# Zero rows and zero weights around the 48 rows of the shift-16 pairs, in a fused three-layer CIN kernel

## The reference

```python
def _L0_rec_ref(inputs, W1, b1, W2, b2, W3, b3, fc_W, fc_b):
    X0 = inputs.reshape(-1, NUM_FIELDS, EMBED_DIM)        # 64 x 32 x 64
    Xi = X0
    pools = []
    for W, b in ((W1, b1), (W2, b2), (W3, b3)):
        out_ch = W.shape[0]                               # 128
        m = Xi.shape[1]                                   # 32, then 128
        Wr = W.reshape(out_ch, NUM_FIELDS, m)
        Xi = jnp.einsum('bhd,bmd,ohm->bod', X0, Xi, Wr) + b[None, :, None]
        pools.append(Xi.sum(axis=-1))
    concat = jnp.concatenate(pools, axis=-1)
    return concat @ fc_W.T + fc_b
```

## Time and profile before

| | |
|---|---|
| median of three runs | 107.69 us |
| the profiled execution's own time | 108.17 us |
| its span in the profile | 106.4 us |
| PE busy | 81.1 us (76%), 303 matmuls |
| DVE busy | 62.7 us (59%) |
| POOL busy | 38.5 us (36%) |
| ACT busy | 34.8 us (33%) |
| chain that ended last | PE 69%, DVE 16%, DMA 5%, ACT 4%, issue 3% |

### The profile page before, as it was taken

The page is one execution under the profiler, slowest core; times in us unless marked ns, Lnnn a source line. Parts: engine busy times, 40 slices in busy tenths (PEclk is TensorE's granted clock), DMA queues, the critical chain, the costliest instruction groups (busy, mean ns, idle before and its releaser), DMA issues.

```text
span 106.4 us, 960 instructions
## 1 busy us (share of the span) xinstructions
PE 81.1 (76%) x303; PEld 60.8 (57%) x303; DVE 62.7 (59%) x87; ACT 34.8 (33%) x66; POOL 38.5 (36%) x31
## 2 busy tenths in 40 slices
PE   0042692006999999934999999999999999999921
PEld 0031570004899879934767766776677666866710
DVE  0239999998600029959995999829987011020072
ACT  4008400019500277462809722076190200201100
POOL 2033099930700079955602309245062204022000
PEclk9999999755555555555589999999999999999998
DMA  3959999920599998971074643700000000000000
GB/s 94 402 135 353 419 431 419 434 117 0 112 110 125 393 404 250 116 310 65 0 219 176 194 200 89 305 3 0 0 6 0 0 0 0 0 0 0 0 0 0
DMA packets 3464, 15.64 MB, mean 147 GB/s; under 512 B 516, under 2 KB 644, under 8 KB 2180
## 3 DMA queue, kind: packets, MB, share of 16 engines
q1 hardware_dynamic: 3460, 15.59, 45.0%
HBM read 14.27 MB, written 0.00 MB: 134 GB/s over the span
## 4 chain that ended last, share of the span: by engine, by line
PE 69%; DVE 16%; DMA 5%; ACT 4%; issue 3%; SPq 0%; DVEq 0%
PE x_ps L538 27%; PE a_ps L538 27%; PE a_ps L599 11%; DMA rep<-xr 5%; DVE w_sb L180 5%; DVE v L476 2%; DVE z_ps L406 2%; ACT feat L313 2%; DVE feat L415 2%; DVE rows_sb L437 1%; PE a_ps L526 1%; ACT v_all L313 1%; ACT a_sb L313 1%; DVE total L509 1%; DVE total L506 1%
## 5 line engine op out<-in xcount | busy, mean ns | idle before, releaser
L538 PE MATMUL x_ps<-feat,w_hi 128*128 128x512 f32 x64 | 27.9, 495 | 2.4 <-DMA fc_all<-fc 2.4
L406 DVE TENSOR_TENSOR z_ps<-rep 128x512 f32<-128x512 f32 x24 | 21.2, 910 | 13.2 <-DMA rep<-xr 12.3
L538 PE MATMUL a_ps<-feat,a_hi 128*128 128x512 f32 x64 | 21.9, 403 | 0.0
L251 POOL TENSOR_TENSOR z_pool<-rep 128x512 f32<-128x512 f32 x8 | 14.9, 1858 | 15.3 <-DMA rep<-xr 13.6
L538 PEld LDWEIGHTS x_ps<-feat,w_hi 128*128 128x128 f32 x64 | 15.1, 236 | 7.0 <-DMA fc_all<-fc 2.8
L313 ACT ACTIVATE feat<-z_ps 128x512 fp32r<-128x512 f32 x24 | 13.9, 592 | 14.1 <-DVE z_ps L406 14.1
L285 POOL TENSOR_TENSOR x<-x 128x512 f32<-128x512 f32 x6 | 8.5, 1413 | 23.5 <-DVE x L466 23.5
L466 DVE SCALAR_TENSOR_TENSOR x<-a_ps,vec,x 128x512 f32<-128x512 f32 x8 | 6.0, 744 | 18.5 <-PE a_ps L538 18.5
L538 PE MATMUL x_ps<-feat,w_lo 128*128 128x512 f32 x32 | 15.6, 488 | 1.6 <-DVE w_tail L456 1.6
L415 DVE TENSOR_TENSOR feat<-z_ps,feat 128x512 fp32r<-128x512 f32 x24 | 16.0, 682 | 1.0 <-ACT feat L313 0.8
L599 PEld LDWEIGHTS a_ps<-v_all,w_sb 128*128 128x128 f32 x60 | 14.6, 331 | 1.6 <-issue 0.9
(11 more groups left out here) (66 smaller groups left out, 69.0 us busy)
## 6 DMA issues: line engine op xcount, KB each, us to landing
rep<-xr SPq DMA_DIRECT2D x8, 1024.0 KB, 5.4
w_sb<-w SPq DMA_DIRECT2D x4, 512.0 KB, 8.8
w_sb<-w SPq DMA_DIRECT2D x2, 1024.0 KB, 13.5
w_sb<-w SPq DMA_DIRECT2D x1, 560.0 KB, 3.8
tail<-z_hi SPq DMA_DIRECT2D x2, 256.0 KB, 5.4
xp<-x SPq DMA_DIRECT2D x1, 512.0 KB, 8.1
lin<-xp_lo SPq DMA_DIRECT2D x1, 512.0 KB, 6.7
xa<-x SPq DMA_DIRECT2D x1, 256.0 KB, 6.9
```

Source lines behind the costliest of these rows:

```text
L251: nc.gpsimd.tensor_tensor(z_pool[:, c % 2, :], rep[:, c % 2, left, :], rep[:, c % 2, right, :], ALU.mult).then_inc(zp_done, 1)
L406: nc.vector.tensor_tensor(z_ps[:, k, :], rep[:, c % 2, left, :], rep[:, c % 2, right, :], ALU.mult).then_inc(z_done, 1)
L538: last = nc.tensor.matmul(bank, w, f, **kw)
```

## The change

The three SBUF tensors of the shift-16 pairs, `tail`, `w1_tail` and `a_tail`, grow from 48 to 128 partitions. POOL writes zeros into all three ahead of its first product. The copies and DMAs of the real data still write rows 0 to 47. The matmuls of L559 and L572 are written as before, over the whole tensors, and so now have 128 rows, 80 of them zero by zero. ACT waits for two of the memsets before it copies a tail weight, SP for all three before its DMAs into `tail`.

```diff
-        tail = sb("tail", [3 * HALF, CHUNKS, N], f32r)
+        tail = sb("tail", [P, CHUNKS, N], f32r)
-        w1_tail = sb("w1_tail", [3 * HALF, M], f32r)
+        w1_tail = sb("w1_tail", [P, M], f32r)
-        a_tail = sb("a_tail", [3 * HALF, M], f32r)
+        a_tail = sb("a_tail", [P, M], f32r)
...
+        tail_zero = sem("tail_zero")
...
                 sp.wait_ge(done, 1)
+                sp.wait_ge(tail_zero, 3)
                 sp.dma_start(tail[row * HALF:(row + 1) * HALF, :, :].bitcast(f32),
...
+            nc.gpsimd.memset(w1_tail[:, :].bitcast(f32), 0.0).then_inc(tail_zero, 1)
+            nc.gpsimd.memset(a_tail[:, :].bitcast(f32), 0.0).then_inc(tail_zero, 1)
+            nc.gpsimd.memset(tail[:, :, :].bitcast(f32), 0.0).then_inc(tail_zero, 1)
             pairs(0)
...
-                copy(tl[:, :], a_ps[1][0:3 * HALF, 0:M]).then_inc(wt_hi, 1)
+                act.wait_ge(tail_zero, 2)
+                copy(tl[0:3 * HALF, :], a_ps[1][0:3 * HALF, 0:M]).then_inc(wt_hi, 1)
```

## The result

The changed kernel takes 102.83 us (median of four runs, 102.33 to 105.63) against 107.97 us before (107.32 to 108.32, four runs). The ratio, taken without the execution of 105.63 us, is 0.9515, with an interval of 0.9442 to 0.9589; the medians differ by 5.1 us. Forecast were 101.9 us and a range of 100.3 to 103.5.

A forecast was written before the change was run, and what follows sets the result against it. From about 55 us on, PE's matmul count times the start-to-start step was taken as the bound. Savings of 5.2 + 0.65 - 0.05 = 5.8 us gave 101.9 us against the median of 107.69, range 100.3 to 103.5.

The forecast's parts named there:

- The tail's price and its cause: PE at the higher clock: each 48-row tail costs 0.40 us extra by draining PE on entry and leaving; padding removes both.
- the end of a group: Rival at PE's tails: the gap belongs to closing a PSUM group, so nothing changes, 107.7 us; chance 0.04.
- The tails at the higher clock, 5.2 us: 14 tails on PE behind the clock's rise: twelve at 0.40 us and two at 0.2 us, together 5.2 us saved.
- The allowance of 0.2 for the tail ahead of L624: Tail at 93.68 us, before L624's one-row matmuls: only 0.2 us saved, since those may charge for the switch themselves.
- The tails at the lower clock, 0.65 us: Two early tails, layer 1 of chunk 1 and L572: 0.7 us of PE time saved, 0.65 us taken as reaching the end.
- each waiting for the one before: Chain behind L572: L599 matmuls, ACT's copies, DVE's rows, transposes and PE follow in turn, passing PE's early gain on.
- The memset, nothing: POOL's three memsets, 3.4 us for `tail`, end at about 5.3 us inside idle time lasting to 7.04 us: no cost.
- The rival's mechanism: A dear memset makes POOL's first product late and DVE's chain slip; chance of costing over a microsecond 0.06.
- The new wait at `a_product(2)`, 0.05 us: PE, come forward, may wait there for DVE's product of chunk 0: 0.35 us at most, 0.05 us taken.
- The sum: Whole kernel: 5.2 + 0.65 - 0.05 = 5.8 us saved, giving 101.9 us against the median.
- the clock's rise: PE's clock rising up to 3 us earlier or later against its work: 100.5 to 103.3 us, most of the range.

The follow-up runs named there:

- middle48: Kernel before with 48-row tails moved inside their group, in the a products and in layer 1 from chunk 2 on: 107.94 us, before 107.57 in that series.
- pad64: Changed kernel with the three tensors 64 rows high instead of 128: 107.95 us.
- memset_only: Changed kernel with its 128-row zeroed tensors, but tail matmuls reading only rows 0 to 47: 107.32 us against 107.31 before, ratio 1.001.
- again: Changed kernel run once more without any edit, for an undisturbed profile: 102.82 us, against 107.31 before in the same series.
- memset3: Changed kernel with the memset of the tail tensor done three times in a row: 106.39 us.
- y_late: Changed kernel with the output's six small matmuls (L624, L625) issued behind the last a product, not ahead of the last layer-1 product: 102.32 us.
- again2: Changed kernel run a third time without any edit, next to a 96-row version: 102.39 us.
- cold48: Changed kernel with the two early tails (layer 1 of chunks 0 and 1) back to 48 rows: 102.85 us.
- a_only: Changed kernel with only the eight tails of the a products at 128 rows, those of layer 1 at 48: 104.42 us.
- rep_early_y_late: As y_late, with SP also issuing the replicas of chunk 2 ahead of its DMAs into tail and xp: 101.27 us, ratio to before 0.9348.

## Why the prediction was right, point by point

**The tail's price and its cause.** Right. 0.40 us a tail was forecast from four steps, and the four steps fell from 1.31 to 0.91 us. The cause, rows and not the end of a group, is shown by `middle48` and `pad64` from both sides, and `memset_only` leaves nothing above its noise for the rest of the change. That it is a drain of PE is the likeliest reading and no more.

**The tails at the higher clock, 5.2 us.** Right. The stretch holds thirteen of the fourteen tails and fell by 4.91 us. The fourteenth, of the layer-1 product of chunk 2, has 0.3 of its 0.40 us ahead of the stretch (0.09 on entry and 0.20 in the step behind): 5.2 us in all. That product itself, 4.81 us before and 4.39 in `again`, measures nothing of the kind: it took from 3.58 (`memset3`) to 5.10 us (`y_late`) with full rows, by where the clock rose. The allowance of 0.2 for the tail ahead of L624 was right too. The step behind this tail fell from 0.42 only to 0.33 us (91.51 to 91.84 in the first trace), not to 0.23, because L624 brings a switch of its own; with the entry that is 0.18.

**The tails at the lower clock, 0.65 us.** This is the term that was mis-sized. The premise, that they would cost 0.7 us of PE's time up to the small matmuls, held: `again2`, at the low rate in the trace from 25 to 45 us like the kernel before, has the clean pattern of 1.28 us around its tails, and its last small matmuls start 0.88 us earlier (44.26 against 45.14), 0.72 of it gained by the end of the two tails (38.43 against 39.15). Before and in `again2`:

```profile
45.14 1.04 PE L599 MATMUL misc_ps<-v_all,w_sb 128*128 128x33 f32 x4
```

```profile
44.26 1.04 PE L605 MATMUL misc_ps<-v_all,w_sb 128*128 128x33 f32 x4
```

What failed is "each waiting for the one before". ACT's copies no longer wait for PE but stand right behind ACT's own feature, which waits for DVE and the replicas:

```profile
44.13 0.60 ACT L318 ACTIVATE feat<-z_ps 128x512 fp32r<-128x512 f32 x1 [1.08 <-DVE z_ps L412]
44.63 0.97 ACT L318 ACTIVATE a_sb<-a_ps 128x495 f32<-128x495 f32 x2
```

In the chain the copies start at 44.73 us against 45.37, so 0.64 of the 0.88 are left. DVE's last low part of chunk 2 then meets POOL's product (45.57 to 46.84 us) and takes longer. Before and in `again2`:

```profile
46.96 0.69 DVE L415 TENSOR_TENSOR feat<-z_pool,feat 128x512 fp32r<-128x512 f32 x1 [1.08 <-ACT feat L313]
```

```profile
46.22 1.17 DVE L421 TENSOR_TENSOR feat<-z_pool,feat 128x512 fp32r<-128x512 f32 x1 [0.33 <-ACT feat L318]
```

It starts 0.74 us earlier and takes 0.48 more, and the transposes start only 0.27 us earlier (49.04 against 49.31). So the term was 0.3 us where PE went at the low rate, on one pair of traces. Where it went faster from 28 to 33 us, the early tails were worth nothing: `pad64` and `cold48`, which have the switches, start their transposes at 49.00 and 48.98 us, `again`, which has not, at 49.01.

**The memset, nothing.** Right: 3.51 us against 3.4 worked out from the slope of two short ones, 1.8 us of cover left. `memset_only` times the whole edit at a ratio of 1.001 (0.9942 to 1.0079). The rival's mechanism is real, as `memset3` shows, but my price for it, microsecond for microsecond, was too low: 3.2 us at the transposes where 1.9 were due.

**The new wait at `a_product(2)`, 0.05 us.** Of the right order, 0 to 0.2 us, depending on where the clock rises. In `again` there is no wait: DVE's product of chunk 0 is over at 60.54 us (59.81 + 0.73) and PE's matmul follows its predecessor in a clean step at 61.17. In `again2` the clock rose earlier and PE was there 0.6 us sooner, while DVE's product ended at 60.56 (59.83 + 0.73). PE's matmul started at 60.62, and this wait is the 0.16 us by which the stretch of `again2` is longer. In `memset3` it cost 0.2 us. So DVE did not come forward with PE there, and a faster PE would meet this limit next.

**The sum.** 5.2 us at the higher clock and 0.3 at the lower make 5.5; against the 5.8 forecast, it is the early tails that are missing. The spans of single traces say less, since the place of the clock's rise is in them: against 106.4 us before, `again` is 5.5 us shorter and `again2` 6.1. The medians give 5.1 in the first series, 4.5 and 5.3 in the two others with this kernel; the kernel before varies from 105.4 to 109.1 us by itself. The traced execution of it, 108.17 us, is a long one with POOL first at 13.2 us; no trace of a short one is kept, so whether the order accounts for these stays open.

**The spread.** The range named the clock's rise as its main part. That is one of two. The other, which I did not see, is the order of DVE and POOL at 13.3 us. That all three medians of this kernel (102.83, 102.82, 102.39) lie inside the range is thus in part luck: no traced execution of it had DVE first, and in the kernels that had it the transposes started more than 1 us earlier.

## What to carry to other kernels

Look at the distance from start to start, not at durations, around a matmul of few rows in a stream of full ones; here each one of 48 or 64 rows cost 0.40 us more at the higher clock, nearly twice a clean step of 0.228, and zero rows cost nothing. Padding to 96 rows was enough. Whether the gain arrives is decided by who stands on the chain at that place: the 14 tails where PE was the chain brought 5.2 us; the two early ones brought PE up to 0.88 us and the end 0.3 at most. Before padding, see that the zeros can be written in idle time, and what would run side by side if they could not.

## What the runs showed of the hardware

*The rate of PE and the granted clock do not always agree.* In `memset_only` the clock is given as 1.00 from 28 to 36 us, with PE busy throughout; in the trace of before it is 0.50 in the same stretch:

```profile
28.00:36.00 8.00, 8.00 (x32) 7.02 (x30) 0.00 (x0) 1.06 (x1) 0.00 (x0) 1.00 1.05 225
```

```profile
28.00:36.00 8.00, 8.00 (x33) 7.33 (x32) 0.41 (x1) 0.00 (x0) 0.46 (x1) 0.50 1.07 171
```

Yet both have the steps of the lower level, 1.28 us for a wide matmul and four small ones (27.37 to 28.65 in `memset_only`). In `again`, with 0.68 us for the same set, the clock is given as 1.00 as well. The steps tell the level, the column did not.

*The same work is clocked differently from run to run.* By its steps, the part from 25 to 45 us ran at the low rate in the traces of before, `again2`, `memset_only`, `a_only`, `memset3`, `y_late` and `rep_early_y_late`, and in part at the high one in the other seven. Kernels with and without padding stand on both sides; `again` and `again2` are the same kernel.

*DVE and POOL on large products.* One operation of DVE over 1024 elements took 1.22 us when it started ahead of POOL's and 3.4 when it started behind it, in all fourteen traces. A subtraction of 512 took 0.68, 1.17, 2.10 or 2.56 us, the longer times where POOL was at work on a product.
